# Five-layer attention kernel: first-layer input normalisation on ScalarE, GpSimd's split reordered behind VectorE's max split

## The chip, the cores and the metric

The kernel runs on one core of one Trainium2 chip. The metric is device time in microseconds (us) of one execution; the time before is the median of 3 runs. Engines: TensorE (PE in the profile; PEld is its weight load), VectorE (DVE), ScalarE (ACT), GpSimd (POOL), SyncE (SP, which here only issues DMAs).

## What is computed

The input x and a context are 16 batches of 128 tokens by 128 channels. Five attention parts follow one another:

```
x = L0(x, ctx)   # layernorm of x and ctx, 8 heads, x + attention
x = L1(x, ctx)   # 16 heads, causal and padding masks, x + attention
x = L2(x, ctx)   # 16 heads, output projection, feed-forward with tanh gelu
x = L3(x, ctx)   # masked self attention, layernorm; cross attention, layernorm; feed-forward, layernorm
```

What the change touches is the first line of the first part, for x and for the context alike:

```
mu = mean(x); var = mean(square(x - mu))
h = (x - mu) * rsqrt(var + 1e-5) * w + b
q = h @ Wq.T + bq        # and k, v from the normalised context
```

## The kernel before, in words

**Units.** The 16 batches are taken in 8 sets of two. A unit `u` is one set in one part: units 0 to 7 are part L0, 8 to 15 L1, and so on to 39. Every unit passes through small steps, and each step has a position relative to its unit (8 positions to a unit, the table `PREPARE` and its companions) and a rank for ties. `schedule` sorts all steps once, and every engine walks the same list and issues those steps that are its own. So the order on each engine is fixed by these tables, and each engine's queue is in order: what stands behind a waiting instruction waits too.

**Steps of a unit in L0.** `ln_in`: VectorE takes statistics of x and context (L678, L682), GpSimd adds epsilon (L513) and raises to the power -1/2 (L516). `ln_norm`: VectorE writes the normalised tokens, four instructions at L705. `ln_tr`: TensorE transposes them (L884), ScalarE applies weight and bias on the way out of PSUM (L572, L575, tiles hT and cnT). `raw_tr`: TensorE transposes the raw tokens (L879), ScalarE copies them (L564, L565, tiles xT and cT). `qk`: TensorE multiplies (L895, L896), ScalarE adds the bias (L584, L585, tile qk_f32). `split`, `rest`, `term1`, `term2`: q and k are cut into three bf16 terms, the first by ScalarE (L596), the others by GpSimd with three subtractions (L521, L523, L527). `stack`: SyncE's DMAs gather products of terms into the tile `pairs` (L427). `score`: TensorE (L849); VectorE takes the row maximum (L745). `nmax`: VectorE cuts the maxima into three bf16 terms, two small subtractions with both inputs in SBUF (L755, L758). `n_tr`: TensorE transposes them (L912), VectorE copies (L761), a DMA lays them beside `pairs` (L443). `attn`: TensorE (L933), ScalarE takes the exponential (L645, tile probs). `pv`: TensorE (L963); `o_evac`: ScalarE (L654, o_sb); `o_tr`: TensorE (L970), VectorE divides (L766, L778). `v`: TensorE (L901), VectorE (L739). `mask`: GpSimd prepares the masks of part L1, four instructions per unit (L474, L476, L479, L483).

**Steady state.** While unit u is attended to, unit u+2 is scored and units u+3 and u+4 are prepared. One such turn of the loop, about 11 us in L0, holds one of each step above, with `score`, `nmax`, `n_tr` and `o_tr` twice (b = 0 and 1 for the two batches of a set).

**The order around the change.** On ScalarE the order in a turn is: qk_f, split, exponential, xT, cT, o_sb, two exponentials, hT, cnT, o_sb, exponential. On GpSimd it is: epsilon, power, the four mask instructions, rest, term1, term2. On VectorE, before anything else of unit 1, the rings for the values are set at `ln_in` of unit 0 (memsets, L692, L693, L696).

```
    L0: (("load", -43), ("ln_in", -32), ("raw_tr", -30), ("ln_norm", -31), ("ln_tr", -26), ("qk", -23),
         ("split", -23), ("rest", -21), ("term1", -19), ("term2", -19), ("v", -16), ("mask", -13)),
```

## Time and profile before

| what | value |
|---|---|
| median of 3 runs | 561.82 us (561.26 to 562.74) |
| the profiled execution: its own time | 558.87 us |
| its span in the profile | 557.1 us |
| PE busy | 486.3 us, 87% of the span |
| DVE busy | 407.6 us, 73% |
| ACT busy | 329.0 us, 59% |
| POOL busy | 263.4 us, 47% |
| mean granted TensorE clock | 0.932 of full speed |

The span runs from the first to the last instruction; the execution's own time is 1.8 us longer, and this execution is 3.0 us under the median. Part L0 fills roughly the first 110 us. Busy shares are averages over stages with different limits, so a change in one stage has to be read in that stage.

### The profile page before, as it was taken

Reading aid. Unit: us, or ns where it says so; the run is one execution under the profiler, and the core shown is the slowest. Engines: PE = TensorE matmul, PEld = TensorE weight load, DVE = VectorE, ACT = ScalarE, POOL = GpSimd, SP = SyncE. Lnnn points to the kernel's source line nnn. Section 1 sums busy time; section 2 is a strip of 40 time slices with the busy share of each in tenths; the row PEclk is TensorE's granted clock in tenths of the full one; section 3 lists DMA queues with packets and bytes.
Section 4 is the critical chain, followed back from the end, with each engine's and each line's share of the span. In section 5 each row is a group of like instructions: output and inputs, shape, how many; then the busy total and the mean of one; then the engine's idle time right before and its main releaser. Section 6 shows DMA issues by size and latency. Waiting matters only on the chain.

```text
span 557.1 us, 16733 instructions
## 1 busy us (share of the span) xinstructions
PE 486.3 (87%) x6464; PEld 299.2 (54%) x6464; DVE 407.6 (73%) x1093; ACT 329.0 (59%) x662; POOL 263.4 (47%) x334
## 2 busy tenths in 40 slices
PE   1548876799999878899999999999999999999973
PEld 1436554455555544455666666565555556666652
DVE  6267876645688886687888877778878897788452
ACT  1424655433556554467777766656666767888851
POOL 3585776824666774524344433334333533422243
PEclk9977889965799996799999999999999999999998
DMA  4593323332233332232223322232333332220000
GB/s 112 99 274 100 103 60 96 81 72 62 64 68 86 76 78 54 59 77 69 69 67 69 69 62 60 54 70 63 77 69 85 80 79 60 69 62 14 13 20 19
DMA packets 72021, 40.68 MB, mean 73 GB/s; under 512 B 7016, under 2 KB 71560, under 8 KB 71816
## 3 DMA queue, kind: packets, MB, share of 16 engines
q1 hardware_dynamic: 71944, 39.61, 30.1%
q8 instruction: 53, 0.87, 0.7%
q14 instruction: 24, 0.20, 0.1%
HBM read 5.00 MB, written 1.05 MB: 11 GB/s over the span
## 4 chain that ended last, share of the span: by engine, by line
PE 65%; POOL 9%; ACT 7%; DVE 6%; SPq 5%; issue 4%; DMA 3%; POOLq 0%; ACTq 0%; DVEq 0%
PE o_ps L963 14%; PE attn_ps L933 12%; PE misc_ps L993 5%; PE misc_ps L984 5%; PE misc_ps L895 5%; PE misc_ps L970 4%; PE misc_ps L901 4%; PE misc_ps L896 3%; PE score_ps L816 3%; PE misc_ps L980 2%; POOL probs L533 2%; PE misc_ps L976 2%; POOL rest L521 2%; PE misc_ps L912 2%; POOL terms L523 2%
## 5 line engine op out<-in xcount | busy, mean ns | idle before, releaser
L745 DVE TENSOR_REDUCE max_words<-score_ps 128x4 f32<-128x512 f32 x288 | 195.8, 685 | 67.7 <-PE score_ps L849 66.1
L645 ACT ACTIVATE probs<-attn_ps 128x512 f32<-128x512 f32 x288 | 169.8, 596 | 110.5 <-PE attn_ps L933 107.2
L963 PE MATMUL o_ps<-probs,v 128*32 128x128 f32 x2304 | 127.0, 294 | 12.6 <-POOL probs L533 8.0
L849 PE MATMUL score_ps<-pairs 52*128 52x128 bf16 (+1 forms) x1152 | 118.7, 226 | 9.1 <-DMA pairs<-terms 9.1
L521 POOL TENSOR_TENSOR rest<-qk_f,terms 128x512 f32<-128x512 f32 x40 | 46.2, 1155 | 162.3 <-ACT terms L596 162.3
L933 PE MATMUL attn_ps<-pairs 55*128 55x128 bf16 (+1 forms) x1152 | 117.8, 225 | 1.9 <-issue 1.0
L933 PEld LDWEIGHTS attn_ps<-pairs 55*128 55x128 bf16 (+1 forms) x1152 | 66.7, 97 | 49.9 <-issue 34.1
L963 PEld LDWEIGHTS o_ps<-probs,v 128*32 128x32 f32 x2304 | 46.3, 110 | 60.0 <-issue 16.9
L849 PEld LDWEIGHTS score_ps<-pairs 52*128 52x128 bf16 (+1 forms) x1152 | 69.8, 98 | 11.0 <-DMA pairs<-terms 9.5
L533 POOL TENSOR_SCALAR_AFFINE_SELECT probs<-probs 128x512 f32<-128x512 f32 x64 | 39.9, 635 | 22.4 <-ACT probs L645 22.4
L527 POOL TENSOR_TENSOR terms<-rest,terms 128x512 bf16<-128x512 f32 x40 | 46.8, 1170 | 1.9
L654 ACT ACTIVATE o_sb<-o_ps 128x256 f32<-128x256 f32 x80 | 30.9, 386 | 27.8 <-PE o_ps L963 27.6
L523 POOL TENSOR_TENSOR terms<-qk_f,terms 128x512 bf16<-128x512 f32 x40 | 46.1, 1153 | 0.0
L970 PE MATMUL misc_ps<-ident,o_sb 128*128 128x128 f32 x160 | 35.0, 302 | 9.8 <-ACT o_sb L654 9.0
L513 POOL TENSOR_SCALAR var_eps<-mean_var 128x2 f32<-128x2 f32 (+1 forms) x32 | 7.1, 222 | 75.7 <-DVE mean_var L682 75.7
L993 PE MATMUL misc_ps<-hidden,w 128*128 128x256 f32 x128 | 34.5, 396 | 1.0 <-ACT hidden L633 1.0
L755 DVE TENSOR_TENSOR max_words<-max_words 128x16 f32<-128x16 f32 (+1 forms) x80 | 31.6, 395 | 2.8
L784 DVE SCALAR_TENSOR_TENSOR xT<-misc_ps,col,xT 128x256 f32<-128x256 f32 x40 | 19.3, 482 | 18.9 <-PE misc_ps L980 13.9
L984 PE MATMUL misc_ps<-xT,w 128*128 128x256 f32 x128 | 31.8, 392 | 0.7 <-DVE xT L800 0.7
L584 ACT ACTIVATE qk_f<-misc_ps,col 128x256 f32<-128x256 f32 x24 | 11.4, 473 | 33.9 <-PE misc_ps L896 33.9
L816 PE MATMUL score_ps<-mask_l,ident_bf 32*32 32x128 bf16 x512 | 31.1, 233 | 0.0
L766 DVE RECIPROCAL recip<-misc_ps 128x16 f32<-128x16 f32 (+1 forms) x80 | 19.3, 241 | 13.9 <-PE misc_ps L970 13.4
(104 smaller groups left out, 766.8 us busy)
## 6 DMA issues: line engine op xcount, KB each, us to landing
pairs<-terms SPq DMA_DIRECT2D x240, 128.0 KB
w<-in_weights_dram SPq DMA_DIRECT2D x1, 1984.0 KB, 8.8
x_tok<-in_x_dram SPq DMA_DIRECT2D x8, 128.0 KB, 3.2
c_tok<-in_ctx_dram SPq DMA_DIRECT2D x8, 128.0 KB, 3.3
pairs<-max_rows SPq DMA_DIRECT2D x64, 12.0 KB
out_dram<-x_tok SPq DMA_DIRECT2D x8, 128.0 KB, 1.8
pairs<-constant_rows SPq DMA_DIRECT2D x4, 112.0 KB
row<-in_rows_dram SPq DMA_DIRECT2D x1, 320.0 KB, 4.4
```

The lines of the kernel that those rows point to most:

```text
L521: pool.tensor_tensor(rest[:, :, :], qk_f32[:, :, :], terms[:, :, 0, :], ALU.subtract)
L523: pool.tensor_tensor(terms[:, :, 1, :], qk_f32[:, :, :], terms[:, :, 0, :], ALU.subtract)\
L533: pool.affine_select(out=probs[n % PROBS_RING][:, :, :], in_=probs[n % PROBS_RING][:, :, :], compare_op=ALU.is_ge, fill=0.0, base=0, patte ...
L645: act.activation(probs[n % PROBS_RING][:, :, :].rearrange("p h q -> p (h q)"), attn_ps[n % 2][:, :], ACT.Exp, scale=float(D // HEADS[part] ...
L745: dve.tensor_reduce(max_words[ub(step) % 2][:, QUAD * g:QUAD * (g + 1)], score_ps[n % 2][:, :].rearrange("p (h k) -> p h k", h=QUAD), AX_X ...
L816: pe.matmul(bank[part_, :].rearrange("p (h n) -> p h n", h=4)[:, :, part_], ident_bf[part_, part_], mask[part_, part_].unsqueeze(1).to_bro ...
L849: return pe.matmul(score_ps[NUM[step] % 2][:, j * S:(j + 1) * S], tile[score_rows(u), QUAD * g + j, 0, b * S:(b + 1) * S], tile[score_rows ...
L933: last = pe.matmul(attn_ps[n % 2][:, j * S:(j + 1) * S], pairs[attn_rows(u), h, 1, b * S:(b + 1) * S], pairs[attn_rows(u), h, 0, b * S:(b ...
L963: last = pe.matmul(o_ps[32 * j:32 * j + 32, region * P:(region + 1) * P], values, probs[n % PROBS_RING][:, j, :], start=part == L0 or g % ...
L970: last = pe.transpose(bank[:, k * P:(k + 1) * P], o_sb[ub(step) % 2][:, k * P:(k + 1) * P], ident[:, :])
L984: last = pe.matmul(bank[:, half * TOK:(half + 1) * TOK], weight(f"w1_{part}_{2 * b + half}"), xT[s][:, :], start=True, stop=True)
L993: last = pe.matmul(bank[:, 0:TOK], weight(f"w2_{part}_{c}"), hidden[:, c, :], start=(c == 0), stop=(c == 3))
```

## The change

Three edits, all for part L0.

1. `PREPARE`: `term1` moves from position -19 to -21, beside `rest`, and `mask` from -13 to -11. `term2` of units 2 to 7 waits until VectorE has finished the max split (L758) of batch 1 of unit u-2.
2. `ln_norm`: VectorE now computes only `shift = -mean * rstd` (one instruction on 128x4 elements), and ScalarE writes the normalised tokens as `rstd * x + shift`, four activations. New tile `shift_ring`, new semaphore `shift_ready`. Two buffers of `normed_in` and of `shift` guard each other as before.
3. The memsets of the value rings stand behind the first shift, no longer behind the first statistics.

```diff
     L0: (("load", -43), ("ln_in", -32), ("raw_tr", -30), ("ln_norm", -31), ("ln_tr", -26), ("qk", -23),
-         ("split", -23), ("rest", -21), ("term1", -19), ("term2", -19), ("v", -16), ("mask", -13)),
+         ("split", -23), ("rest", -21), ("term1", -21), ("term2", -19), ("v", -16), ("mask", -11)),
...
                 if step.kind == "term2":
                     pool.wait_ge(split2_done, u + 1)
+                    if 2 <= u < SETS:
+                        pool.wait_ge(maxterms_ready, ub(the("nmax", u - 2, 1)) + 1)
                     pool.tensor_tensor(terms[:, :, 2, :], rest[:, :, :], terms[:, :, 1, :], ALU.subtract)\
...
+                if kind == "ln_norm":
+                    n = LN_STEPS.index(the("ln_in", u))
+                    act.wait_ge(shift_ready, u + 1)
+                    if u >= 2:
+
+                        evacuated(act, the("ln_tr", u - 2))
+                    srcs = [t[s][:, k, :] for t in (x_tok, c_tok) for k in range(PAIR)]
+                    for k, src in enumerate(srcs):
+                        last = act.activation(normed_in_ring[u % 2][:, k, :], src, ACT.Identity,
+                                              scale=rstd_ring[n % LN_RING][:, k:k + 1],
+                                              bias=shift_ring[u % 2][:, k:k + 1])
+                    last.then_inc(input_normed, 1)
...
-                if kind == "ln_in" and u == 0:
+                if kind == "ln_norm":
+                    n = LN_STEPS.index(the("ln_in", u))
+                    dve.wait_ge(rstd_ready, n + 1)
+                    if u >= 2:
+
+                        dve.wait_ge(input_normed, u - 1)
+                    dve.scalar_tensor_tensor(shift_ring[u % 2][:, :], mean_var_ring[n % LN_RING][:, 0:2 * PAIR, 0],
+                                             -1.0, rstd_ring[n % LN_RING][:, 0:2 * PAIR], ALU.mult, ALU.mult)\
+                        .then_inc(shift_ready, 1)
+                if kind == "ln_norm" and u == 0:
 
                     for ring in range(RING):
                         dve.memset(v8[ring][:, :], 1.0)
...
-                if kind == "ln_norm":
-                    n = LN_STEPS.index(the("ln_in", u))
-                    dve.wait_ge(rstd_ready, n + 1)
-                    if u >= 2:
-
-                        evacuated(dve, the("ln_tr", u - 2))
-                    srcs = [t[s][:, k, :] for t in (x_tok, c_tok) for k in range(PAIR)]
-                    for k, src in enumerate(srcs):
-                        last = dve.tensor_scalar(normed_in_ring[u % 2][:, k, :], src,
-                                                 mean_var_ring[n % LN_RING][:, k, 0:1],
-                                                 rstd_ring[n % LN_RING][:, k:k + 1], ALU.subtract, ALU.mult)
-                    last.then_inc(input_normed, 1)
```

**ScalarE, a turn of the steady loop in L0, before**: from the last exponential of one turn to the first of the next.

```order
L654 ACTIVATE o_sb<-o_ps 128x256
L645 ACTIVATE probs<-attn_ps 128x512
L584 ACTIVATE qk_f<-misc_ps,col 128x256
L585 ACTIVATE qk_f<-misc_ps,col 128x256
L596 ACTIVATE terms<-qk_f 128x2x256
L645 ACTIVATE probs<-attn_ps 128x512
L564 ACTIVATE xT<-misc_ps 128x256
L565 ACTIVATE cT<-misc_ps 128x256
L654 ACTIVATE o_sb<-o_ps 128x256
```

**The same place of ScalarE in the changed kernel** (its lines: L670 is o_sb, L661 the exponential, L578 the new normalisation, L600, L601 and L612 are qk_f and the split).

```order
L670 ACTIVATE o_sb<-o_ps 128x256
L661 ACTIVATE probs<-attn_ps 128x512
L578 ACTIVATE normed_in<-x_tok,shift,rstd 128x128 x2
L578 ACTIVATE normed_in<-c_tok,shift,rstd 128x128 x2
L600 ACTIVATE qk_f<-misc_ps,col 128x256
L601 ACTIVATE qk_f<-misc_ps,col 128x256
L612 ACTIVATE terms<-qk_f 128x2x256
L661 ACTIVATE probs<-attn_ps 128x512
```

The four activations of the next unit's normalisation stand in front of qk_f, the split and the exponential of this turn.

**GpSimd, the same turn, before**: epsilon, power, masks, then the three subtractions.

```order
L513 TENSOR_SCALAR var_eps<-mean_var 128x4
L516 TENSOR_TENSOR rstd<-var_eps,minus_half 128x4
L474 TENSOR_SCALAR mask_rows_l<-valid_raw 4x256
L476 TENSOR_SCALAR mask_l<-valid_raw 128x256
L479 AFFINE_SELECT mask_rows_l<-mask_rows_l 4x256
L483 AFFINE_SELECT mask_l<-mask_l 128x256
L521 TENSOR_TENSOR rest<-qk_f,terms 128x512
L523 TENSOR_TENSOR terms<-qk_f,terms 128x2x256
L527 TENSOR_TENSOR terms<-rest,terms 128x2x256
```

**The same turn of GpSimd in the changed kernel** (L523 is rest there, L525 term1, L531 term2).

```order
L515 TENSOR_SCALAR var_eps<-mean_var 128x4
L518 TENSOR_TENSOR rstd<-var_eps,minus_half 128x4
L523 TENSOR_TENSOR rest<-qk_f,terms 128x512
L525 TENSOR_TENSOR terms<-qk_f,terms 128x2x256
L476 TENSOR_SCALAR mask_rows_l<-valid_raw 4x256
L478 TENSOR_SCALAR mask_l<-valid_raw 128x256
L481 AFFINE_SELECT mask_rows_l<-mask_rows_l 4x256
L485 AFFINE_SELECT mask_l<-mask_l 128x256
L531 TENSOR_TENSOR terms<-rest,terms 128x2x256
```

The first two subtractions now come ahead of the masks, and the third, with its new wait, behind them. On VectorE the four normalisation instructions of each turn become one; TensorE and SyncE keep their order.

## Rows read from the trace of the kernel before

**Rows 1.** The page: span, TensorE's granted clock in 40 slices, a DMA issue.

```profile
span 557.1 us, 16733 instructions
...
PEclk9977889965799996799999999999999999999998
...
w<-in_weights_dram SPq DMA_DIRECT2D x1, 1984.0 KB, 8.8
```

**Rows 2.** Waits of PE, 0 to 140 us: us in total, times, longest us.

```profile
PE misc_ps L912 <- DVE max_words L758: 8.9, 9, 1.5
```

**Rows 3.** Chain that ended last, 0 to 150 us: start us, us, what.

```profile
33.88 7.01 DMA pairs<-terms
...
42.29 0.96 PE misc_ps L901 x4
...
86.34 0.45 PE misc_ps L901 x4
```

**Rows 4.** Timeline of DVE, 76 to 87 us: start us, us, instruction, [idle before].

```profile
79.28 0.78 DVE L705 TENSOR_SCALAR normed_in<-x_tok,mean_var,rstd 128x128 f32<-128x128 f32 x2 [0.50 <-POOL rstd L516]
...
83.02 1.51 DVE L755 TENSOR_TENSOR max_words<-max_words 128x8 f32<-128x8 f32 x1
```

**Rows 5.** Timeline of POOL, 76 to 87 us.

```profile
78.20 1.04 POOL L516 TENSOR_TENSOR rstd<-var_eps,minus_half 128x4 f32<-128x4 f32 x1
79.33 1.07 POOL L474 TENSOR_SCALAR mask_rows_l<-valid_raw 4x256 bf16<-4x256 uint8 x1
...
83.36 1.14 POOL L523 TENSOR_TENSOR terms<-qk_f,terms 128x512 bf16<-128x512 f32 x1
```

**Rows 6.** Timeline of ACT, 76 to 87 us.

```profile
78.29 0.47 ACT L584 ACTIVATE qk_f<-misc_ps,col 128x256 f32<-128x256 f32 x1 [3.34 <-PE misc_ps L896]
...
79.76 0.58 ACT L645 ACTIVATE probs<-attn_ps 128x512 f32<-128x512 f32 x1
80.23 0.38 ACT L564 ACTIVATE xT<-misc_ps 128x256 f32<-128x256 f32 x1
80.50 0.39 ACT L565 ACTIVATE cT<-misc_ps 128x256 f32<-128x256 f32 x1
...
83.26 0.56 ACT L572 ACTIVATE hT<-misc_ps,col 128x256 f32<-128x256 f32 x1
83.71 0.56 ACT L575 ACTIVATE cnT<-misc_ps,col 128x256 f32<-128x256 f32 x1
```

**Rows 7.** Timeline of PE, 76 to 87 us.

```profile
81.41 0.41 PE L970 MATMUL misc_ps<-ident,o_sb 128*128 128x128 f32 x2 [0.27 <-ACT o_sb L654]
...
84.88 0.22 PE L912 MATMUL misc_ps<-ident_bf,max_words 128*24 128x128 bf16 x1 [1.48 <-DVE max_words L758]
```

**Rows 8.** Timelines of DVE and POOL, 101 to 104 us: a max split beside a mask instruction.

```profile
102.19 0.17 DVE L755 TENSOR_TENSOR max_words<-max_words 128x8 f32<-128x8 f32 x1
...
101.83 0.85 POOL L476 TENSOR_SCALAR mask_l<-valid_raw 128x256 bf16<-128x256 uint8 x1
```

**Rows 9.** Timeline of SP's queue, 28 to 35 us.

```profile
28.41 0.47 SPq L390 DMA_DIRECT2D w<-in_weights_dram  x1
28.92 5.68 SPq L427 DMA_DIRECT2D pairs<-terms  x6
```

**Rows 10.** Timelines of POOL and ACT, 91 to 96 us: end of L0.

```profile
91.95 1.15 POOL L527 TENSOR_TENSOR terms<-rest,terms 128x512 bf16<-128x512 f32 x1
...
95.46 0.47 ACT L584 ACTIVATE qk_f<-misc_ps,col 128x256 f32<-128x256 f32 x1
```

**Rows 11.** Busy time and granted clock (PEclk), 120 to 128 us.

```profile
120.00:128.00 8.00, 8.00 (x65) 4.44 (x63) 4.40 (x13) 1.58 (x3) 0.02 (x1) 0.50 0.15 34
```

**Rows 12.** Timeline of DVE in L1: the first nmax of two units apart, three times.

```profile
119.92 0.18 DVE L755 TENSOR_TENSOR max_words<-max_words 128x16 f32<-128x16 f32 x1
...
149.84 0.63 DVE L755 TENSOR_TENSOR max_words<-max_words 128x16 f32<-128x16 f32 x1
...
172.34 1.10 DVE L755 TENSOR_TENSOR max_words<-max_words 128x16 f32<-128x16 f32 x1
```

More of the change, by code:

```diff
@@ L231, in build @@
         rstd_ring = [sb(f"rstd{r}", [P, 2 * PAIR]) for r in range(LN_RING)]
+        shift_ring = [sb(f"shift{r}", [P, 2 * PAIR]) for r in range(2)]
         normed_in_ring = [sb(f"normed_in{r}", [P, 2 * PAIR, D]) for r in range(2)]
@@ L295, in build @@
         input_normed = sem("input_normed")
+        shift_ready = sem("shift_ready")
         split1_done = sem("split1_done")
```

## The prediction

> **What bounds the kernel now.** The page came first: its clock row shows that TensorE is not at full speed in the first third [rows 1], and the change lies wholly in L0, in the first 110 us, so the rest is read only for what moves with it. Second came TensorE's waits [rows 2]: the transposes of the maxima (L912) stood 8.9 us, in nine waits, for VectorE's L758. Third the chain of waits [rows 3]: in L0 it runs through the loop, and each turn can be measured from the end of one L901 to the end of the next. The first ends at 42.29 + 0.96 = 43.25, the fifth at 86.34 + 0.45 = 86.79, so four turns take 43.54 us, 10.9 us each. Last came one turn in the timelines, 76 to 87 us [rows 4 to 7].
>
> The reader is to see two halves in that turn. In the first, ScalarE takes qk_f at 78.29 as soon as TensorE has it, the exponential follows at 79.76, 1.47 us later, and o_sb reaches TensorE's L970 at 81.41, 1.65 us after the exponential began [rows 6, 7]. ScalarE is in the path here: xT, cT and o_sb follow the exponential back to back. In the second half VectorE comes from L970 to the max split at 83.02, 1.61 us later, and this instruction on 8 elements takes 1.51 us [rows 4]. It ends at 84.53, when GpSimd's term1 (L523) has ended at 84.50 [rows 5]; TensorE has stood 1.48 us for it [rows 7]. From L912 at 84.88 to the end of L901 at 86.79 are 1.91 us.
>
> **The change part by part.**
>
> *The max split is freed.* GpSimd's order becomes rest, term1, masks, term2. A split that meets no subtraction takes 0.17 us, and so it does beside the mask instruction L476 [rows 8]. With L758 (0.2 us behind it) and 0.14 us to TensorE, L912 starts 0.52 us after an undisturbed L755 starts. In the turn shown it started 84.88 - 83.02 = 1.86 us after it. Saved: 1.34 us, in each of four turns (the stalls are 1.41 to 1.56 us). The new wait of term2 costs nothing: masks of 2.9 us stand in front of it, and VectorE will be done before they are. Behind term2 on GpSimd stand epsilon and power of the next unit, whose statistics come later still. The DMAs that wait for term2 have more than a turn before TensorE needs them.
>
> *The normalisation moves to ScalarE and stands in front of qk_f.* This is the large term. It can begin only after the shift, and the shift only after the power. VectorE began L705 at 79.28, just as the power ended (78.20 + 1.04 = 79.24) [rows 4, 5]. So the shift runs at 79.28, takes about the 0.17 us of another tiny VectorE instruction [rows 8], and ScalarE starts the four activations at about 79.5. At that time qk_f, the split and the exponential would already have been running for 1.2 us; now they wait in the queue. What four such activations take is not in the trace. Nearest are L572 and L575, which also have a scale and a bias from memory: 0.45 us apart for 256 elements [rows 6]. An exponential of 512 elements takes 0.58 us and a copy of 256 takes 0.38, so 128 elements fewer save 0.10. That makes 0.35 us each and 1.4 us for four. The low bound is the plain copies, 0.27 us apart, less 0.10: 0.17 each, 0.7 us. The high bound is 0.47 us each with no overlap (L584's length): 1.9 us. I take 1.4, from the row with the same operands.
>
> The Trainium skill has a table for this ("VectorE: DVE Perf Modes", section on the TRN2 errata): 224 + 128 cycles at 1.2 GHz for a ScalarE instruction from SBUF, an estimate of 1.17 us for four. By it the sum below would be 0.9 us less; no row here shows the operation.
>
> qk_f then starts at 79.5 + 1.4 = 80.9 instead of 78.29: 2.6 us late. Everything behind it keeps its distances: exponential 82.37, L970 84.02, L755 85.63, L912 86.15. Before, L912 was at 84.88. **Net +1.27 us for this turn**: 2.6 late, 1.34 saved. The other three turns have the same shape, and the same steps give 1.27 to 1.29. Four turns: **+5.1 us**. VectorE's relief of four instructions (1.3 us a turn) gains nothing, since in that time it would only wait longer for L970.
>
> *Start.* Memsets behind the first shift let the first unit be normalised about 4 us earlier. But the chain before the first turn is SyncE's issue and the landing of unit 1's products at 33.88 + 7.01 = 40.89 [rows 3]. Those DMAs stand behind 1984 KB of weights issued at 28.41 that take 8.8 us [rows 1, 9]. Unit 1 loses too: its statistics now follow the memsets, its normalisation blocks qk_f of unit 0, and that of unit 2 blocks qk_f of unit 1. I work out term2 of unit 1 about 1 us later, term1 about 2 us earlier. The landing is set by the bytes in the queue: 0, with bounds of -1.0 (the first products are no longer held for term1) and +0.5.
>
> *End of L0.* In the last turn the masks now stand between term1 and term2 of unit 7, so term2 ends at about 96.0 instead of 93.1, and qk_f of unit 8, at 95.46 before, waits for it [rows 10]: +0.6. The max split there is freed of some 0.2. Together +0.4 us.
>
> **Sum**: 5.1 + 0 + 0.4 = **+5.5 us**. On the profiled execution, 558.87 us of its own time with a span of 557.1, that gives 564.4. It ran 2.95 us under the median; on the median 561.82 it gives **567.3 us**. With the bounds (activations 0.7 to 1.9 us, so -2.8 to +2.0; start -1.0 to +0.5) the forecast's own range is 563.5 to 569.8.
>
> **The rivals.**
>
> *TensorE's clock comes back (ends faster).* From about 119 to 146 us TensorE is busy without a break at a granted 0.50 of full speed, the 1.2 GHz level [rows 11]. It fell after a stage with short waits of TensorE. VectorE's first nmax of units two apart are 29.9 us apart there (119.92 to 149.84) and 22.5 us afterwards (149.84 to 172.34) [rows 12], so this stretch costs 7.4 us. If the new rhythm ahead of it lets the clock stay up, the sum is 5.5 - 7.4 = -1.9: 559.9 us. It decides from 7.2 us of the 7.4 on, or less with cheap activations (557.1 with the low bound). For it: the clock fell three times in L0 behind waits for the max split and not in the fourth turn, so small shifts matter. Against: TensorE's idle time in a turn grows by about 1.3 us.
>
> *The same stretch grows by a unit.* One more unit at the low level costs 7.4 / 2 = 3.7 us: 571.0.
>
> *The mask instruction holds the port (the edit doesn't do what it says).* By the hand count the max split at 85.63 meets L474, which would run from about 84.9 to 85.9. The row with L476 speaks against a stall [rows 8]. If L474 held VectorE up until its own end, 0.3 us a turn, or until L476's end, 1.2 us, the time would be 568.5 to 572.1. The Trainium skill says so ("SBUF — State Buffer", section "Who interferes with whom"): a VectorE instruction with two SBUF inputs contends with a GpSimd instruction that reads SBUF, for that instruction's whole length. The trace agrees for the subtractions and not for L476.
>
> *The delay is largely hidden.* Activations at the low bound, the start's 1.0 and a higher clock during the loop's own matmuls (L901 took 0.96 to 0.45 us): +5.5 - 2.8 - 1.0 - 0.5 = +1.2: 563.0, no change.
>
> **How the numbers follow.** A measurement of this kernel can tell about 0.3%, 1.7 us, from no change. Chances: forecast 0.48; port held 0.07; stretch longer 0.07; these are slower, 0.62. Hidden 0.14: the same. Clock back 0.24: faster. The range of 558.0 to 571.0 takes in the forecast's own and both clock cases; cases of both signs are in it because the clock alone can outweigh the sum.
>
> **What would show it.** Right: in L0 ScalarE shows a wait for the shift of about 1 us or more and then four activations in front of each qk_f, for four turns; qk_f starts 2 to 3 us after TensorE has it ready; TensorE's wait for L758 at L912 almost gone, and one of over 2 us for the exponential in its place; turns of about 12.2 us. Wrong: L755 still over 1 us; activations under 0.25 us apart; the first turn beginning more than 1 us before 43 us; the clock row from 112 to 150 us different from before, in which case the time beyond L0 moves by itself.

## The result and the profile after

The changed kernel takes **574.4 us** (median of four runs, 568.0 to 578.9) against 561.9 for the kernel before: a ratio of 1.020, with a 95% interval of 1.010 to 1.029. It is slower, by 12.5 us where 5.5 were predicted, and 3.4 us above the range (the fastest of the four executions, at 568.0, lies inside it). Executions that stood apart from the others of their kernel are left out of the ratios, here and in the table below, so that a ratio can differ from the quotient of the medians. The profiled execution took 577.5 us of its own time, 3.1 over its median, while that of before lay 3.0 under its own; so the two traces are 18.7 us apart in span, and the differences read from them are those of one execution of each kernel.

The page of the changed kernel, to be read against [rows 1]:

```profile
span 575.8 us, 16753 instructions
...
PEclk9986777855689998796999999999999999999998
...
L976 PE MATMUL o_ps<-probs,v 128*32 128x128 f32 x2304 | 129.9, 300 | 19.2 <-ACT probs L661 9.8
```

One slice is 14.4 us here. From slice 4, at 43 us, through slice 11 no digit is above 8; before, slices 7 and 8 were at 9. TensorE's idle time in front of L976 is put down to the exponential.

For the comparison each kernel is cut at the evictions of the values, v(0) to v(23): the starts of VectorE's `v<-misc_ps` (L739 before, L752 now). The turns forecast in the prediction are v(2) to v(6). This small table is worked out from those rows of both timelines.

| stretch | before, us | after, us | difference |
|---|---|---|---|
| start to v(2) | 43.29 | 43.63 | +0.3 |
| v(2) to v(6), four turns of L0 | 43.54 | 54.78 | **+11.2** |
| v(6) to v(7) | 9.77 | 9.51 | -0.3 |
| v(7) to v(11), end of L0 and start of L1 | 54.37 | 60.26 | **+5.9** |
| v(11) to the end | 406.1 | 407.6 | +1.5 |

TensorE's waits from v(2) to v(6), to be read against [rows 2] (us in total, times, longest us):

```profile
PE misc_ps L925 <- ACT qk_f L601: 9.3, 3, 3.1
PE o_ps L976 <- ACT probs L661: 6.3, 4, 3.5
PE misc_ps L983 <- ACT o_sb L670: 1.2, 4, 0.3
```

The wait for the max split (5.8 us in four times between v(2) and v(6) of before) is gone, as predicted, and two waits for ScalarE have taken its place: L925, the transposes of the maxima, now waits until ScalarE has taken qk_f, and L976 for the exponential. One turn, v(3) at 57.35 to v(4) at 71.04, answers to [rows 4 to 7]. First VectorE and ScalarE:

```profile
60.51 0.16 DVE L711 SCALAR_TENSOR_TENSOR shift<-mean_var,rstd 128x4 f32<-128x4 f32 x1 [0.50 <-POOL rstd L518]
60.70 0.88 ACT L578 ACTIVATE normed_in<-x_tok,shift,rstd 128x128 f32<-128x128 f32 x2 [3.90 <-DVE shift L711]
61.49 0.87 ACT L578 ACTIVATE normed_in<-c_tok,shift,rstd 128x128 f32<-128x128 f32 x2
62.27 0.46 ACT L600 ACTIVATE qk_f<-misc_ps,col 128x256 f32<-128x256 f32 x1
...
63.71 0.58 ACT L661 ACTIVATE probs<-attn_ps 128x512 f32<-128x512 f32 x1
...
67.45 0.35 DVE L768 TENSOR_TENSOR max_words<-max_words 128x8 f32<-128x8 f32 x1
```

and TensorE in the same turn:

```profile
57.86 0.59 PE L909 MATMUL misc_ps<-cnT,w 128*128 128x256 f32 x2
...
63.13 0.28 PE L925 MATMUL misc_ps<-ident_bf,max_words 128*24 128x128 bf16 x1 [3.10 <-ACT qk_f L601]
64.34 0.66 PE L976 MATMUL o_ps<-probs,v 128*32 128x128 f32 x8 [0.93 <-ACT probs L661]
65.59 0.66 PE L983 MATMUL misc_ps<-ident,o_sb 128*128 128x128 f32 x2
...
67.60 1.06 PE L897 MATMUL misc_ps<-ident,normed_in 128*128 128x128 f32 x4
...
70.14 0.41 PE L983 MATMUL misc_ps<-ident,o_sb 128*128 128x128 f32 x2 [0.29 <-ACT o_sb L670]
```

The reader is to see three things. ScalarE waits 3.90 us for the shift while the input of qk_f is ready, since TensorE's L909 ended at 58.45; the four activations take 62.27 - 60.70 = 1.57 us. The exponential follows qk_f after 1.44 us. And after its waits of 3.10 and 0.93 us TensorE runs long: L976 takes 0.66 us (0.42 ahead of the waits, at 58.39), L983 0.66 against 0.41 [rows 7]. The windows of the turn (us, busy time of PE, PEld, DVE, ACT, POOL with counts, granted clock, DMA share, GB/s) show the clock beside it:

```profile
57.30:63.10 5.80, 2.73 (x31) 1.96 (x28) 3.70 (x17) 2.38 (x6) 1.27 (x2) 0.94 0.36 92
63.10:70.10 7.00, 5.74 (x52) 3.66 (x52) 2.63 (x8) 4.65 (x11) 5.55 (x7) 0.56 0.30 79
```

The granted clock is 0.56 in the seven microseconds behind the waits: nearly all of them at the 1.2 GHz level. TensorE is then 82% busy, and the chain of waits runs through it.

### The profile page after: what moved, and what is told of

Its sections match the earlier page's. It is cut to its first block, busy times and chain, and to the rows that moved or that the text cites. A ratio compares the mean times of both kernels' runs of the same rounds, so it can differ in the third digit from the quotient of the medians.

```text
span 575.8 us, 16753 instructions
## 1 busy us (share of the span) xinstructions
PE 498.9 (87%) x6464; PEld 306.1 (53%) x6464; DVE 393.3 (68%) x1069; ACT 342.2 (59%) x694; POOL 263.4 (46%) x334
## 4 chain that ended last, share of the span: by engine, by line
PE 66%; POOL 12%; ACT 9%; DVE 6%; issue 4%; DMA 2%; SPq 0%; POOLq 0%; ACTq 0%; DVEq 0%
PE o_ps L976 15%; PE attn_ps L946 13%; PE misc_ps L1006 5%; PE misc_ps L997 5%; PE misc_ps L983 5%; PE misc_ps L908 4%; PE misc_ps L914 3%; PE score_ps L829 3%; PE misc_ps L909 3%; PE misc_ps L993 2%; PE misc_ps L989 2%; POOL probs L537 2%; POOL rest L523 2%; PE score_ps L862 2%; POOL terms L531 2%
## 5 line engine op out<-in xcount | busy, mean ns | idle before, releaser
L758 DVE TENSOR_REDUCE max_words<-score_ps 128x4 f32<-128x512 f32 x288 | 195.8, 685 | 78.3 <-PE score_ps L862 76.5
L661 ACT ACTIVATE probs<-attn_ps 128x512 f32<-128x512 f32 x288 | 170.0, 597 | 115.5 <-PE attn_ps L946 111.6
L976 PE MATMUL o_ps<-probs,v 128*32 128x128 f32 x2304 | 129.9, 300 | 19.2 <-ACT probs L661 9.8
L523 POOL TENSOR_TENSOR rest<-qk_f,terms 128x512 f32<-128x512 f32 x40 | 46.2, 1156 | 192.2 <-ACT terms L612 192.2
L862 PE MATMUL score_ps<-pairs 52*128 52x128 bf16 (+1 forms) x1152 | 122.8, 232 | 6.4 <-DMA pairs<-terms 6.4
L946 PE MATMUL attn_ps<-pairs 55*128 55x128 bf16 (+1 forms) x1152 | 120.8, 229 | 2.3 <-DVE max_words L758 1.1
L946 PEld LDWEIGHTS attn_ps<-pairs 55*128 55x128 bf16 (+1 forms) x1152 | 68.3, 98 | 52.7 <-issue 36.3
L976 PEld LDWEIGHTS o_ps<-probs,v 128*32 128x32 f32 x2304 | 47.1, 112 | 67.1 <-ACT probs L661 19.9
L862 PEld LDWEIGHTS score_ps<-pairs 52*128 52x128 bf16 (+1 forms) x1152 | 72.9, 100 | 9.1 <-DMA pairs<-terms 7.0
L531 POOL TENSOR_TENSOR terms<-rest,terms 128x512 bf16<-128x512 f32 x40 | 46.6, 1165 | 1.3
L670 ACT ACTIVATE o_sb<-o_ps 128x256 f32<-128x256 f32 x80 | 30.9, 387 | 26.2 <-PE o_ps L976 25.9
L525 POOL TENSOR_TENSOR terms<-qk_f,terms 128x512 bf16<-128x512 f32 x40 | 46.2, 1155 | 0.0
L983 PE MATMUL misc_ps<-ident,o_sb 128*128 128x128 f32 x160 | 36.7, 314 | 8.7 <-ACT o_sb L670 7.9
L925 PE MATMUL misc_ps<-ident_bf,max_words 128*48 128x128 bf16 (+1 forms) x80 | 19.7, 246 | 10.1 <-ACT qk_f L601 9.3
L578 ACT ACTIVATE normed_in<-x_tok,shift,rstd 128x128 f32<-128x128 f32 x16 | 7.1, 489 | 35.7 <-DVE shift L711 35.7
```

The lines of the kernel that those rows point to most:

```text
L523: pool.tensor_tensor(rest[:, :, :], qk_f32[:, :, :], terms[:, :, 0, :], ALU.subtract)
L531: pool.tensor_tensor(terms[:, :, 2, :], rest[:, :, :], terms[:, :, 1, :], ALU.subtract)\
L661: act.activation(probs[n % PROBS_RING][:, :, :].rearrange("p h q -> p (h q)"), attn_ps[n % 2][:, :], ACT.Exp, scale=float(D // HEADS[part] ...
L758: dve.tensor_reduce(max_words[ub(step) % 2][:, QUAD * g:QUAD * (g + 1)], score_ps[n % 2][:, :].rearrange("p (h k) -> p h k", h=QUAD), AX_X ...
L862: return pe.matmul(score_ps[NUM[step] % 2][:, j * S:(j + 1) * S], tile[score_rows(u), QUAD * g + j, 0, b * S:(b + 1) * S], tile[score_rows ...
L946: last = pe.matmul(attn_ps[n % 2][:, j * S:(j + 1) * S], pairs[attn_rows(u), h, 1, b * S:(b + 1) * S], pairs[attn_rows(u), h, 0, b * S:(b ...
```

## The experiments

Two theories stood at the start. **Queue**: the extra time is queueing behind the four activations, plus whatever I mis-sized of it. **Clock**: the queueing is as predicted, and the rest is TensorE running at half speed behind its own longer wait. Twelve kernels were run. The table has the comparison with runs of the kernel before in the same call, the four turns v(2) to v(6), the stretch v(7) to v(11), and the mean granted clock in that stretch (from 30 windows each). The turns, the stretch and the clock are those of one profiled execution of each kernel. The kernel before itself varied (see the last section).

| kernel | median us | before beside it | ratio, 95% | four turns | v(7) to v(11) | clock there |
|---|---|---|---|---|---|---|
| before | | | | 43.5 | 54.4 | 0.72 |
| after | 574.4 | 561.9 | 1.020 (1.010 to 1.029) | 54.8 | 60.3 | 0.60 |
| e1 order only | 563.4 | 560.1 | 1.008 (1.000 to 1.015) | 43.5 | 59.3 | 0.65 |
| e2 normalisation only | 578.5 | 560.1 | 1.034 (1.027 to 1.041) | 54.4 | 56.1 | 0.70 |
| e3 memsets only | 562.2 | 562.0 | 1.010 (1.005 to 1.016) | 44.7 | 54.4 | 0.72 |
| e4 late normalisation | 562.0 | 560.1 | 1.006 (0.997 to 1.014) | 38.4 | 60.1 | 0.60 |
| e5 some matmuls added | 576.0 | 560.1 | 1.031 (1.024 to 1.037) | 52.5 | 57.5 | 0.79 |
| e6 as e4, old order | 563.8 | 562.0 | 1.012 (1.006 to 1.019) | 44.0 | 53.3 | 0.78 |
| e7 as e4, no new wait | 561.9 | 562.0 | 1.011 (1.004 to 1.018) | 38.3 | 60.1 | 0.60 |
| e8 more matmuls added | 573.2 | 562.0 | 1.030 (1.024 to 1.036) | 49.6 | 55.1 | 0.97 |
| e9 e4, matmuls at the end | 560.8 | 562.0 | 1.006 (1.001 to 1.011) | 40.7 | 58.6 | 0.85 |
| e10 before, same matmuls | 563.9 | 562.0 | 1.015 (1.006 to 1.024) | 43.7 | 57.8 | 0.82 |
| e11 e4, old order at the end | 566.0 | 560.8 | 1.016 (1.006 to 1.026) | 41.2 | 59.8 | 0.60 |
| e12 after, old order at the end | 577.3 | 560.8 | 1.037 (1.028 to 1.047) | 57.9 | 57.4 | 0.64 |

**The parts alone.** e1 has only GpSimd's part:

```diff
-("term1", -19), ... ("mask", -13)
+("term1", -21), ... ("mask", -11)
                 if step.kind == "term2":
                     pool.wait_ge(split2_done, u + 1)
+                    if 2 <= u < SETS:
+                        pool.wait_ge(maxterms_ready, ub(the("nmax", u - 2, 1)) + 1)
```

> Edit 1 alone: GpSimd's new order and the new wait of term2, normalisation left on VectorE, memsets where they were. Queue theory (the loss comes from the normalisation standing in front of qk_f on ScalarE, the reorder is a gain): the max split falls from 1.4 to 1.56 us to under 0.4 us, each of four turns in L0 gets about 1.3 us shorter (10.9 to 9.6 us), total 555 to 558 us. Rival (the new wait or the later masks cost): turns stay at 10.9 us or grow, total 562 or more.

The split's stall is gone, but the four turns take 43.50 us as before: 9.73, 12.18, 9.90 and 11.69. They alternate. In the long ones VectorE's first normalisation instruction, which e1 leaves on VectorE, takes 2.30 us. It runs beside two subtractions of GpSimd, which the new order has put there; in the short turn behind it takes 0.60 (the third row), and the pair of instructions 2.0 us instead of 3.0:

```profile
55.92 2.30 DVE L707 TENSOR_SCALAR normed_in<-x_tok,mean_var,rstd 128x128 f32<-128x128 f32 x2 [0.51 <-POOL rstd L516]
58.14 0.81 DVE L707 TENSOR_SCALAR normed_in<-c_tok,mean_var,rstd 128x128 f32<-128x128 f32 x2
...
68.11 0.60 DVE L707 TENSOR_SCALAR normed_in<-x_tok,mean_var,rstd 128x128 f32<-128x128 f32 x2 [0.51 <-POOL rstd L516]
...
55.86 1.16 POOL L521 TENSOR_TENSOR rest<-qk_f,terms 128x512 f32<-128x512 f32 x1
56.98 1.16 POOL L523 TENSOR_TENSOR terms<-qk_f,terms 128x512 bf16<-128x512 f32 x1
```

xT, behind it in VectorE's queue, and the maxima come late, and TensorE waits for both:

```profile
59.34 0.66 PE L886 MATMUL misc_ps<-ident,normed_in 128*128 128x128 f32 x4 [0.99 <-DVE xT L782]
61.68 0.27 PE L914 MATMUL misc_ps<-ident_bf,max_words 128*24 128x128 bf16 x1 [1.28 <-DVE max_words L760]
```

The granted clock is still 1.00 when this begins (57.0 to 59.4 us), and the mean clock of the four turns, 0.78, 0.84, 0.85 and 0.79, doesn't tell the long from the short. So the expectation of a gain missed, and the numbers that came are those of its rival (turns of 10.9 us on average, a total of 562 or more) with another cause than it named: **the collision with GpSimd's subtractions moves from the max split to the normalisation.** In e4 and e7 below, with the same order and the normalisation on ScalarE, the turns behind the first are all alike at 9.3 us. The order edit alone gains nothing; it needs the normalisation off VectorE.

e2 has only the normalisation (the DVE block of `ln_norm` replaced by the shift, the four activations in ACT's, as in the change).

> Edit 2 alone: normalisation on ScalarE in front of qk_f, GpSimd's order and the memsets as before. Queue theory: qk_f starts about 2.8 us late in each turn and the split stall stays, since rest and term1 follow the later split too: turns of 14 us or more, total 575 to 582 us. Rival (the loss is made by the combination, the reorder delaying GpSimd): total within 3 us of before, 559 to 565 us.

The total is a hit; the turns are 13.37 to 13.70 us, shorter than the 14 expected and nearly those of the whole change (13.68 to 13.72), and the expected stall of the split is not there (no L766 over 0.34 us in the loop). **At the clock of these turns the order edit therefore adds nothing to a turn that has the normalisation in front of qk_f.** The reason is in e2's GpSimd and VectorE timelines:

```profile
62.18 1.16 POOL L523 TENSOR_TENSOR rest<-qk_f,terms 128x512 f32<-128x512 f32 x1 [0.38 <-ACT terms L610]
63.30 1.16 POOL L525 TENSOR_TENSOR terms<-qk_f,terms 128x512 bf16<-128x512 f32 x1
64.53 1.16 POOL L529 TENSOR_TENSOR terms<-rest,terms 128x512 bf16<-128x512 f32 x1
```

```profile
65.74 0.17 DVE L766 TENSOR_TENSOR max_words<-max_words 128x8 f32<-128x8 f32 x1
```

The slow TensorE brings the split at 65.74, just after the last subtraction ended at 65.69. The old order frees it too. At full clock it might not: in e8 below the split comes 9.62 us after the value eviction, and by the distances of e2's rows the third subtraction of the old order would run from 8.87 to 10.03 us behind it. No run has that combination.

e3 moves only the memsets:

```diff
-                if kind == "ln_in" and u == 0:
+                if kind == "ln_norm" and u == 0:
```

(behind the normalisation of unit 0, which stays on VectorE).

> Only the value memsets move, behind the normalisation of unit 0, which stays on VectorE; GpSimd's order and the turns of the loop stay as before. Queue theory: the first units' chain starts up to 1.0 us earlier or 0.5 us later, the turns stay at 10.7 to 11.3 us, the total within 1.5 us of before run beside it (ratio 0.997 to 1.003). Rival (the 2.8 us per turn come from the memsets' new place, through the start of the loop): turns over 12 us. Rival (any change of the first 40 us moves where TensorE's granted clock falls): the total moves by over 2 us with turns like before's.

v(2) is reached at 44.77 us, 1.48 later than before, outside the 0.5 allowed, and the four turns take 1.2 us more. The medians are 0.3 us apart, but the ratio of 1.010 lies outside the 0.997 to 1.003 expected, so this expectation missed, and a cost of the memsets' new place of some us in the total (1% is 5.6) is not excluded. The +11.2 us of the four turns is not theirs: e2, with the memsets where they were, has them too.

**The clock in the turn.** e5 and e8 are the changed kernel with matmuls added where TensorE waits; their results are not read. e5 has four of 256 columns ahead of the first transposes of the maxima (`n_tr`, which the expectations call the normed transpose) of a unit, e8 seven and two more:

```diff
+                if kind == "n_tr" and b == 0 and 1 <= u < SETS:
+                    for _ in range(7):
+                        pe.matmul(o_ps[:, 2 * P:4 * P], ident[:, :], w[:, 0:2, :]...)
```

(and the same with `range(2)` behind those transposes.)

> The changed kernel with four extra matmuls of 256 columns on TensorE (into unused columns of o_ps, the result is never read) in each L0 turn just before it waits for qk_f; nothing else differs. Clock theory (about 1.3 us of each turn's loss is TensorE at half clock behind its long wait, and more at the end of L0): the granted clock in L0 rises, the stretch from the exponential to the end of the transposes of normed_in falls from 4.3 to about 3 us, turns of 12.3 us instead of 13.7, total 5 to 10 us under the changed kernel. Rival (the clock does not matter, the chain is ScalarE's): turns stay at 13.7 us or grow by the extra work, total as changed or above.

> The changed kernel with 7 more matmuls of 256 columns ahead of the first normed transpose of a unit and 2 ahead of the second, results not read, units 1 to 7: they fill TensorE's two new waits. Clock theory (the 1.4 us per turn beyond the 12.2 us of the prediction are TensorE's granted clock falling behind its own waits): the granted clock stays near 1.00 from 49 to 100 us and all four turns measure 12.0 to 12.6 us; the total falls by at most 6 us against the changed kernel, and by less if the clock falls earlier in what follows (568 to 577). Rival (the extra is queueing on ScalarE and VectorE, not the clock): turns stay at 13.5 to 14 us with the clock at 1.00. Rival (the added matmuls are late themselves): turns over 13 us with TensorE busy where it waited.

e5 kept the clock at 1.00 behind the waits in one turn (from 48 us to its end), and that one took 12.19 us; the others took 13.1 to 13.6, with the clock at 0.50 from 66.0 to 69.5 us in the next. The total did not fall, so its expectation was half missed. e8 held it in three full turns (the first took 13.02 us, at 0.83 in its first half, where 12.0 to 12.6 was expected of all four), here in its windows:

```profile
56.30:68.40 12.10, 11.28 (x108) 8.36 (x106) 6.42 (x27) 7.20 (x17) 6.24 (x9) 1.00 0.35 90
68.40:80.60 12.20, 11.39 (x110) 8.46 (x108) 6.52 (x27) 7.20 (x17) 7.73 (x11) 1.00 0.27 67
80.60:92.80 12.20, 11.39 (x110) 8.47 (x108) 6.53 (x27) 7.20 (x17) 7.40 (x10) 1.00 0.27 68
```

and ScalarE and TensorE do in them what they did without the additions:

```profile
71.80 0.88 ACT L578 ACTIVATE normed_in<-x_tok,shift,rstd 128x128 f32<-128x128 f32 x2 [3.91 <-DVE shift L711]
72.59 0.86 ACT L578 ACTIVATE normed_in<-c_tok,shift,rstd 128x128 f32<-128x128 f32 x2
73.36 0.45 ACT L600 ACTIVATE qk_f<-misc_ps,col 128x256 f32<-128x256 f32 x1
```

(L875 is added matmuls)

```profile
71.67 2.54 PE L875 MATMUL o_ps<-w,ident 128*128 128x256 f32 x11
74.22 0.23 PE L929 MATMUL misc_ps<-ident_bf,max_words 128*24 128x128 bf16 x1
```

ScalarE waits for the shift as long as ever (3.91 against 3.90) and the activations take as long (1.56). qk_f comes 4.91 us after the value eviction, against 4.92, and the transposes of the maxima 5.77 us after it, against 5.78. Up to there the two kernels run alike; behind it only the clock differs, and the turns take 12.19 us instead of 13.69. **The clock's share of a turn here is 1.5 us; the queue's is what was predicted, within 0.3 us.** The rival of queueing falls. The total of e8 is 1.2 us lower only, inside the expected range and less than the executions of either kernel differ by. Its trace shows where the rest went: with the added matmuls the next two turns take 12.73 and 21.56 us, 9.51 and 16.54 without. Behind them, from v(8) to v(11), where nothing is added, e8 runs at a clock of 1.00 and takes 33.5 us, with TensorE busy for 28.1; the changed kernel takes 43.7 there (busy 41.0, clock 0.62) and the kernel before 42.1 (39.6, 0.64), all with the same 429 matmul records. By this the low clock costs 10.2 us in these three turns in the changed kernel and 8.6 in the kernel before.

**Where the normalisation stands.** e4, e6 and e7 put the activations into a step of their own, behind the third exponential of a turn:

```diff
-("ln_norm", -31), ("ln_tr", -26)
+("ln_norm", -31), ("ln_act", -28), ("ln_tr", -26)
-                if kind == "ln_norm":
+                if kind == "ln_act":
```

> The whole change, but ScalarE's four normalisation instructions are issued three positions later, behind the exponential of the turn's third quad, where ScalarE was idle for 1 us. Queue theory: the work is the same, only its place differs, so qk_f is on time again; turns of 9.6 to 10.2 us, total 554 to 560 us. Rival (ScalarE has too much work, 1.6 us a turn more, wherever it stands): turns of over 11.5 us, total above 566 us.

> The normalisation on ScalarE in a step of its own behind the third exponential, GpSimd's order and waits as before the change. If the gain of the run with the whole change and the late normalisation (turns of 9.3 to 10.4 us against 10.9) came from the freed maximum split, the split's stall of 1.4 to 1.6 us is back here and the turns are 10.4 to 11.2 us. If it came from taking the four normalisations off VectorE, turns stay below 9.8 us. Total, by either: 556 to 565, since the loop's gain is given back where TensorE's clock falls between the fifth turn and layer 1; a total under 552 would say that the clock gives nothing back.

> The late normalisation on ScalarE with the new GpSimd order, but without the wait for the maximum split. If the wait alone keeps the split free, the split's stall is back (over 1 us in each turn) and turns are 10.2 to 11.0 us; if the new order already does it, the stall stays under 0.5 us and turns are 9.3 to 9.6 us. Total 556 to 565 by the same reasoning as the run beside it.

Three of e4's four turns are 9.31 us at a clock of 1.00 (the first 10.43 at 0.80), below the 10.9 of before and below the 9.6 to 10.2 expected; the total of 562.0 is above the 554 to 560 expected. The same four instructions, now in ScalarE's idle time (they end at 59.40, hT follows at 60.22):

```profile
54.39 0.47 ACT L600 ACTIVATE qk_f<-misc_ps,col 128x256 f32<-128x256 f32 x1 [1.70 <-PE misc_ps L909]
...
57.77 0.87 ACT L578 ACTIVATE normed_in<-x_tok,shift,rstd 128x128 f32<-128x128 f32 x2
58.54 0.86 ACT L578 ACTIVATE normed_in<-c_tok,shift,rstd 128x128 f32<-128x128 f32 x2
59.31 0.57 ACT L661 ACTIVATE probs<-attn_ps 128x512 f32<-128x512 f32 x1
```

At full clock, then, the place in front of qk_f costs 12.19 - 9.31 = **2.88 us** a turn, and the clock 1.50 more. e6, the same with the old order, has the stall back and turns of 10.7 to 11.6 us, the last above the 11.2 expected; e7 has the new order without the new wait, is free of the stall and has e4's turns. Both totals lie where they were expected. Four turns of e6 take 44.0 us, where the kernel before takes 43.5: off VectorE alone the normalisation gains nothing either. Their max splits, one turn each, e6 first:

```profile
70.48 1.43 DVE L766 TENSOR_TENSOR max_words<-max_words 128x8 f32<-128x8 f32 x1
```

```profile
70.28 0.17 DVE L766 TENSOR_TENSOR max_words<-max_words 128x8 f32<-128x8 f32 x1
```

So with the normalisation out of the way of both VectorE and qk_f the order frees the split and is worth (44.0 - 38.4) / 4 = **1.4 us** a turn; the new wait of term2 does nothing that these turns show. A second pair agrees: the first two turns of e10 below, which up to there is the kernel before, run at a clock of 1.00 and take 10.72 and 10.69 us, 1.4 over e4's 9.31. In e7 the mask instructions run at 69.34 to 71.38, over both splits, without holding them:

```profile
69.34 1.07 POOL L476 TENSOR_SCALAR mask_rows_l<-valid_raw 4x256 bf16<-4x256 uint8 x1
70.49 0.89 POOL L478 TENSOR_SCALAR mask_l<-valid_raw 128x256 bf16<-128x256 uint8 x1
```

**The end of L0.** e4 reaches v(7) 5.9 us before the kernel before, and gives 5.7 back by v(11): its total is the same. In e4's windows the clock falls earlier than in before's (second fence):

```profile
96.00:108.00 12.00, 9.87 (x77) 6.16 (x77) 6.84 (x16) 4.11 (x9) 9.13 (x15) 0.64 0.31 72
108.00:120.00 12.00, 11.84 (x91) 6.70 (x93) 5.52 (x15) 3.71 (x8) 3.42 (x3) 0.50 0.36 84
```

```profile
96.00:108.00 12.00, 8.12 (x105) 5.46 (x103) 8.20 (x23) 6.14 (x13) 10.14 (x16) 1.00 0.38 90
108.00:120.00 12.00, 10.72 (x104) 6.58 (x104) 6.37 (x19) 4.58 (x10) 6.18 (x6) 0.82 0.49 104
```

That the lower clock is where the time goes is seen in the whole stretch v(7) to v(11), which has the same 532 matmul records in both kernels. These are the sums of the windows over it, before first, then the changed kernel:

```profile
sum 54.37, PE 48.03 PEld 27.33 DVE 32.43 ACT 22.96 POOL 29.74; mean PE 1.60 PEld 0.91 DVE 1.08 ACT 0.77 POOL 0.99
sum 60.26, PE 54.74 PEld 31.40 DVE 33.48 ACT 23.82 POOL 29.77; mean PE 1.82 PEld 1.05 DVE 1.12 ACT 0.79 POOL 0.99
```

TensorE is busy for 6.7 us more with the same instructions, and idle for 0.8 us less. So the 5.9 us are not a longer wait. What makes the clock fall sooner is the question that is left, and four kernels went after it. e9 adds matmuls, results not read, in units 5 to 7 of e4 (four ahead of the second product of exponentials and values, L976; two ahead of each transpose of the maxima); e10 has them in units 6 and 7 of the kernel before.

> The whole change with the normalisation on ScalarE in a late step of its own (turns of 9.3 us), and matmuls whose results are not read (256 columns each) where TensorE waits in the units before the granted clock falls: 4 ahead of the second attention product and 2 ahead of each normed transpose of units 5, 6 and 7. Clock theory (the loop's gain of 5.9 us was given back because the clock fell at 94 us instead of 112): the clock stays at 1.00 to past 105 us, the stretch from the eighth to the twelfth value eviction takes 52 to 57 us instead of 60.1, and the total is 550 to 557, 1 to 2% under before beside it. Rival (the stretch is long by its own waits, whatever the clock): it takes 59 to 62 us with the clock at 1.00. Rival (the clock falls all the same, a turn later): 57 to 60 us, total 556 to 562.

> The kernel before with the same added matmuls in units 6 and 7 alone. Clock theory: the stretch from the eighth to the twelfth value eviction, 54.4 us before with the clock at 0.50 from 112 to 146 us, takes 48 to 53 us with less of it at 0.50; total 552 to 560. Rival (the matmuls add their own time and the clock falls as before): 55 to 57 us, total 562 to 566.

Both missed. The clock did hold longer (1.00 up to 120 us in e9, 0.85 over the stretch), but the stretch took 58.6 and 57.8 us. The numbers of e9 (58.6, a total of 560.8) are those of its last rival, that the clock falls all the same; the total of e10 (563.9) is that of its rival, that the matmuls add their own time, with a stretch 0.8 us above it. The added matmuls are too large for this test: in the turn after 95 us of e9 they take 1.99 + 1.08 + 1.08 us where e4's TensorE had waits of 1.65 and 0.77. So the two runs don't tell what makes the clock fall.

In the changed kernel, e1, e4 and e7, all with the new order, ScalarE has one wait that the kernel before lacks, near v(7); this is e4's.

```profile
ACT qk_f L600 <- POOL terms L531: 0.8, 1, 0.8
```

This is the predicted +0.6 at the end of L0, at 0.8 us. The four stretches with it take 59.3 to 60.3 us, those of before, e2, e3 and e6 without it 53.3 to 56.1. e11 and e12 took it out, with the old order for units 6 and 7 alone in e4 and in the changed kernel:

```diff
         for kind, pos in PREPARE[part]:
+            if part == L0 and u >= 6:
+                pos = {"term1": -19, "mask": -13}.get(kind, pos)
```

> The whole change with the normalisation in a late step of its own, and GpSimd's table as before the change for units 6 and 7 alone. Theory (the new order is late at the end of layer 0: with the masks of unit 6 between the second and the third subtraction of unit 7, ScalarE's qk_f of unit 8 waits 0.8 us for the latter, TensorE's wait for the exponential grows to 1.65 us, and the granted clock falls 8 us earlier for it): the 0.8 us wait is gone, turns of 9.3 us stay up to unit 6, the clock stays at 1.00 past 100 us, the stretch from the eighth to the twelfth value eviction takes 53 to 56 us instead of 60.1, and the total is 553 to 558, 1% under before beside it. Rival (the clock falls early because the loop itself ran faster, whatever GpSimd's order): 58 to 60 us with the clock at 0.50 before 100 us, total 559 to 564.

> The change as it is, with GpSimd's table as before the change for units 6 and 7 alone. Same theory: the stretch from the eighth to the twelfth value eviction takes 55.5 to 57.5 us (56.1 with the normalisation alone) instead of 60.3, the four turns before it stay at 13.7 us, and the total is 569.5 to 573. Rival: 59 to 61 us and 573 to 577.

The wait is gone in both. In e11 the stretch took 59.8 us at a mean of 0.60 all the same, and the total was 566.0: the clock can fall there without that wait, so it is not the whole cause. In e12 the stretch took 57.4 us, inside what the theory gave, but the total was 577.3, above theory and rival. Whether the wait has a part in it is open.

The two runs show one thing more. Up to v(5) their order is that of e4 and of the changed kernel, instruction for instruction. Still e11's two turns from v(3) to v(5) take 10.3 us at a clock of 0.83, where e4's take 9.31 at 1.00, and e12's three from v(2) take 14.2 to 14.5 us at 0.62 to 0.76, where the changed kernel's take 13.7 at 0.69 to 0.75. So the clock, and with it a turn, differs between executions of the same order, by 0.5 to 1.0 us a turn here, and a single trace doesn't give the clock's share to better than that.

## Why the prediction was wrong

The sign and the queueing held; the size did not, since the lower clock behind a longer wait was left out.

- *Normalisation in front of qk_f*: "2.6 late" per turn. Read from the traces, qk_f starts 4.92 us after the value eviction, where in the turn shown of before it started 78.29 - 76.13 = 2.16 us after it: 2.76 late. In whole turns at full clock it is 2.88, e8 against e4. Its parts: four activations 1.57 us where I took 1.4 from the row with the same operands. Right, 0.3 us small. The formula of the Trainium skill ("VectorE: DVE Perf Modes", section on the TRN2 errata), by which I estimated 1.17 us, is further off: this trace has the four in 1.57 us.
- *The max split is freed*: "saved 1.34". Measured 1.4, e6 against e4. But it isn't a term of its own, as I had it: e1, the order alone, gains 0.0 us in four turns, since the subtractions then meet the normalisation on VectorE, and e2 shows none within the changed kernel's turn, which without the order edit is as long. In the sum at full clock the two terms meet what e8 measures: forecast 12.2, measured 12.19. That it is so close is in part luck, since the cost came out 0.3 larger and the step from before's 10.88 to 9.31 us 0.2 larger than forecast.
- *TensorE's clock in the turn* is the **step that failed**. I carried every instruction behind qk_f with the distances of the turn before ("Everything behind it keeps its distances"), which is a turn at full clock from 79 us on [rows 6, 7], though TensorE's wait ahead of them became 3.10 + 0.93 us. The page of before [rows 1] had shown low digits in the turns of L0. Measured: 0.56 of full clock behind the wait, and 1.50 us a turn in this execution. The four turns cost +11.2 us instead of +5.1: 2.81 a turn instead of 1.27.
- *The rival "clock comes back"* used the right resource with the wrong sign. I wrote against it that TensorE's idle time in a turn grows, and gave that no price. The rival of one more slow unit, +3.7 us at 571.0, was the near one; it is what the stretch v(7) to v(11) shows, at 5.9 us, but it had no part for the turns.
- *Start*: forecast 0, measured +0.3; with the memsets alone moved (e3) +1.5, outside the bound of +0.5.
- *End of L0*: forecast +0.4. The wait of 0.8 us is there, in the turn v(6) to v(7), which is 0.3 us shorter than before; but v(7) to v(11) grew by 5.9, for which the sum had no term. By the busy times above it is the same work at a lower clock. The stretches of the kernels without added matmuls follow the clock in them, but for one pair: 53.3 us at 0.78, 54.4 at 0.72, 56.1 at 0.70, 57.4 at 0.64, 59.3 at 0.65, 59.8 to 60.3 at 0.60. What makes it fall there sooner in one kernel than in another is open, since e11 has the low clock without the wait that I named.
- *The mask instruction holds the port*: the wrong rival. The Trainium skill ("SBUF — State Buffer", section "Who interferes with whom") would have a VectorE instruction with two SBUF inputs contend with any GpSimd instruction that reads SBUF. By the rows of e7 the split takes 0.17 us beside both mask instructions, and 0.35 us in the changed kernel; beside the subtractions it takes 1.4 to 2.5. The trace has the contention for the subtractions, and none of it for the masks beyond that 0.35.

The turn of the changed kernel taken apart by the runs is 9.31 us (order and a late normalisation, e4) + 2.88 (place, e8 less e4) + 1.50 (clock, the changed kernel less e8) = 13.69 us. The kernel before stands at 10.88, or 10.7 in the turns of e10 at full clock, 1.4 over the first: the split's stall. Its first two turns take 10.7 and 10.8 us at a clock of 0.81 and 0.82 as well, so the low clock costs little there, where TensorE would wait for the split in any case.

## What to carry to other kernels

When an edit lengthens a wait of TensorE, price the instructions behind the wait at the lower clock level as well, with the durations that the same trace shows there, and put that case into the range. When a unit is moved to an idle engine, its place in that engine's queue matters more than its length: the same 1.57 us cost 2.9 us a turn more in front of qk_f, with a dependency that comes late, than behind the third exponential. And two edits may not be summed one by one if one changes what the other collides with: here the order alone gained 0.0 us, the late normalisation alone lost 0.5, and both together gained 5.2 us in four turns.

## What was not expected of the hardware

- The kernel before, unchanged, ran from 550.9 to 569.0 us in the course of this study, with a mean granted clock of 0.969 in the fastest and 0.910 in the slowest, and twice at 634 and 638 us with a clock of 0.64. The prediction took 0.3% as what can be told from no change; differences of 1 to 2 us between totals above tell nothing.
- A faster loop is not a faster kernel here: e4 and e7 save 5 us in four turns and end at the median of before, because the clock is lower in what follows: from v(7) to v(11) e4's TensorE is busy for 54.6 us, against 48.0 before, with the same 532 matmul records.
- A shift of 4 elements with two SBUF inputs took 0.16 us in the changed kernel and 1.12 us in e7, where it ran beside a subtraction of GpSimd:

```profile
57.73 1.12 DVE L709 SCALAR_TENSOR_TENSOR shift<-mean_var,rstd 128x4 f32<-128x4 f32 x1 [0.50 <-POOL rstd L518]
...
57.67 1.15 POOL L523 TENSOR_TENSOR rest<-qk_f,terms 128x512 f32<-128x512 f32 x1
```
